# State-space phase of a four-block network: preparation of the next image re-ordered over the steps and partly turned into products on PE, and VectorE's product with C placed between the halves of the next scan

## The reference, cut to what matters

```python
xz = einsum('blc,ec->ble', layer_norm(x), W_in)      # 64 -> 256
xi, z = split(xz)                                     # 128 each
xc = silu(conv_b + sum_k pad(xi)[:, k:k+L] * conv_w[:, k])   # 4 taps along the 1024 positions
dt, Bm, Cm = split(einsum('bld,ed->ble', xc, W_x))    # 4, 16, 16 columns
delta = softplus(einsum('blr,dr->bld', dt, W_dt) + b_dt)
for each position t:                                  # state 128 x 16 per image
    h = h * exp(delta_t * A) + (delta_t * xc_t) * B_t
    y_t = sum over the 16 states of h * C_t
y = (y + xc * Dp) * silu(z)
out = einsum('bld,cd->blc', y, W_out) + x
```

## Time and profile before

| | |
|---|---|
| median of 3 runs | 3678.57 us |
| the profiled execution, its own time | 3668.06 us |
| its span on the core | 3666.4 us |
| busy: PE, DVE, POOL, ACT | 3163.0, 2573.4, 2214.4, 2006.1 us |
| mean granted clock of PE | 0.948 of full |
| first scan of the state-space phase | 2553.05 us into the span |

### The profile page before, as it was taken

One profiled execution on the slowest core, in us unless ns is written; L12 is line 12 of the kernel. 1 busy time (PEld: TensorE's weight loads), 2 busy tenths in 40 slices (PEclk: granted clock), 3 DMA queues, 4 the chain that ended last, 5 costly groups with the idle time before them and its releaser, 6 DMA issues. The chain is left out here.

```text
span 3666.4 us, 55668 instructions
## 1 busy us (share of the span) xinstructions
PE 3163.0 (86%) x18550; PEld 1183.9 (32%) x18550; DVE 2573.4 (70%) x3346; ACT 2006.1 (55%) x2381; POOL 2214.4 (60%) x684
## 2 busy tenths in 40 slices
PE   6999999999999999999995899774888888887787
PEld 2333333333333333333331233341322222222222
DVE  5777777777767777777771222142888988988988
ACT  3566666666656666666663333223555564565554
POOL 0577777777777777777776000003657666666666
PEclk7899999999999999999998999886989999999999
DMA  2000000000000000000003211114333433443443
GB/s 103 12 16 10 16 16 16 16 13 16 16 17 10 16 16 16 19 10 16 16 10 74 92 69 46 48 64 149 119 132 128 155 142 120 153 150 118 147 150 115
DMA packets 74739, 234.86 MB, mean 64 GB/s; under 512 B 13088, under 2 KB 14180, under 8 KB 74420
## 3 DMA queue, kind: packets, MB, share of 16 engines
q1 hardware_dynamic: 69460, 215.06, 17.3%
q0 software_dynamic: 5056, 16.83, 1.3%
HBM read 192.42 MB, written 39.39 MB: 63 GB/s over the span
## 5 line engine op out<-in xcount | busy, mean ns | idle before, releaser
L526 DVE TENSOR_REDUCE at_pmax<-at_ring 128x1 f32<-128x512 f32 x2048 | 1300.8, 685 | 392.0 <-PE at_ring L334 381.2
L479 ACT ACTIVATE at_probs<-at_sc 128x1024 f32<-128x1024 f32 x1024 | 992.5, 1021 | 531.7 <-PE at_sc L402 529.7
L580 POOL TENSOR_TENSOR at_prob_sums<-at_prob_sums,at_probs 128x2048 f32<-128x2048 f32 x256 | 1159.0, 4527 | 74.8 <-ACT at_probs L479 54.5
L398 PE MATMUL at_sc<-at_QT,at_KT 32*128 32x512 f32 x4096 | 782.5, 634 | 4.1 <-issue 3.7
L1634 POOL TENSOR_TENSOR ss_drive<-ss_du,ss_bsb 128x1024 f32<-128x1024 f32 x261 | 610.7, 2352 | 263.9 <-DVE ss_state L1591 257.1
L1534 ACT ACTIVATE ss_decay<-ss_delta,ss_a 128x512 f32<-128x512 f32 x520 | 354.5, 687 | 447.6 <-DVE ss_state L1587 299.5
L410 PE MATMUL at_O<-at_probs,at_V 128*32 128x512 f32 x4096 | 535.3, 606 | 52.5 <-DVE at_att L549 51.6
L580 POOL TENSOR_TENSOR at_prob_sums<-at_probs 128x2048 f32<-128x2048 f32 x64 | 290.7, 4543 | 403.1 <-ACT at_probs L479 403.1
L1423 PE MATMUL ss_Y<-ss_seen,ss_ident 128*128 128x512 f32 x1032 | 520.7, 628 | 0.0
L334 PE MATMUL at_ring<-at_KH,at_QH 32*128 32x512 bf16 x2048 | 442.3, 387 | 5.7 <-DVE at_pmax L526 2.9
L1599 DVE TENSOR_TENSOR ss_seen<-ss_state,ss_C 128x1024 f32<-128x1024 f32 x259 | 316.3, 1221 | 80.4 <-PE ss_C L1411 72.6
(11 more groups left out here) (199 smaller groups left out, 2695.6 us busy)
## 6 DMA issues: line engine op xcount, KB each, us to landing
ss_bsb<-scratch_rows SPq DMA_DIRECT2D x265, 512.0 KB, 6.9
scratch_attn<-at_att SPq DMA_DIRECT2D x64, 256.0 KB, 2.0
fc_att<-scratch_attn SPq DMA_DIRECT2D x32, 512.0 KB, 5.8
ss_xn<-scratch_xm SPq DMA_DIRECT2D x34, 256.0 KB, 5.6
at_xn<-scratch_xn SPq DMA_DIRECT2D x32, 256.0 KB, 3.8
ss_xw<-scratch_xw SPq DMA_DIRECT2D x17, 256.0 KB, 3.9
ln_x<-in_x SPq DMA_DIRECT2D x8, 512.0 KB, 4.2
scratch_xn<-ln_xn POOLq DMA_DIRECT2D x8, 512.0 KB, 3.0
```

The lines of the kernel that those rows point to most:

```text
L398: nc.tensor.matmul(sc[:, h, :], KT[head(h), par, blk(kb)], QT[head(h), par, hs(half)], start=True, stop=False)
L479: nc.scalar.activation(probs[:, kb, two, :].rearrange("p h q -> p (h q)"), sc[:, two, :].rearrange("p h q -> p (h q)"), ACT.Exp, scale=SCA ...
L526: nc.vector.tensor_reduce(pmax[:, quad // 2, h, quad % 2:quad % 2 + 1], ring[:, unit[3], :], AX_X, ALU.max, negate=True).then_inc(max_done, 1)
L580: nc.gpsimd.tensor_tensor(prob_sums[:, half, :, :], before, probs[:, k, :, :], ALU.add).then_inc(pool_sums, 1)
```

## The change

Preparation of image b+1 in the new order (PE: AT_X 5, AT_BC 7, AT_LESS_HI 8, AT_LESS_MID 9, AT_DT 11, AT_Z 13; ACT: AT_PRE 5, AT_U 6, AT_HI 7, AT_MID 8, AT_LOW 9, AT_ABS 11, AT_LN 12, AT_GATE 14; SP writes B at 10, POOL makes delta and du at 13):

- `unit` 1 now makes B and C, `unit` 2 makes delta's input with one 128-row product by `w_delta` = W_x (dt columns) times W_dt, which PE computes once at the start, and `unit` 3 makes z.
- The second and third bf16 parts of B and C are made by PE and ACT: `take_away` repeats the product for B and C and subtracts, with `less` (minus the identity, bf16), the parts that `bc` already holds; ACT copies what is left (`take_mid`, `take_low`). DVE's `take_rest`, ACT's copies of dt and of a second middle part, and POOL's `low` are gone.
- `gate` is made apart from `u_in`, with its own table loads. Softplus is split over ACT's steps 11 and 12.
- DVE runs `see` of step n-1 between the two half scans of step n; Y times gate comes after step 1.
- PE makes the output in two halves, after its steps 1 and 2; ACT still takes it after its decay of step 3.
- The constants are loaded by SP at the end of the loads of the whitening phase; in the state-space phase DVE clears 3 columns of `xn` and the whole of `bc`.

```diff
-def whitening_phase(nc, sem, x_d, total, pair_m, mask_m, ident_m, centred, wm):
+def whitening_phase(nc, sem, x_d, total, pair_m, mask_m, ident_m, centred, wm, load_next):
...
                     sp.dma_start(x[:, u, :], xv[bass.ds(2 * i + u, 1)].rearrange("a p s -> (a p) s")).then_inc(x_in[u], DMA)
+            load_next(sp)
...
+def load_state_space_constants(sp, consts, loaded, w_inT, conv_w, conv_b, w_xT, w_dtT, b_dt, a_log, d_p, w_outT,
+                               select_m, ident_m):
+    w_in, cw, cols, w_x, w_dt, a_neg, w_out, select, ident = consts
+    sp.dma_start(w_in[0:C, :], w_inT).then_inc(loaded, DMA)
+    sp.dma_start(ident[:], ident_m).then_inc(loaded, DMA)
...
-        AT_X, AT_CONV, AT_Z, AT_BC, AT_REST, AT_MID, AT_DT, AT_LOW, AT_DELTA = 6, 6, 8, 9, 10, 11, 12, 12, 13
+        AT_X, AT_BC, AT_LESS_HI, AT_LESS_MID, AT_DT, AT_Z = 5, 7, 8, 9, 11, 13
+        AT_PRE, AT_U, AT_HI, AT_MID, AT_LOW, AT_ABS, AT_LN, AT_GATE = 5, 6, 7, 8, 9, 11, 12, 14
+        AT_ROWS, AT_DELTA = 10, 13
...
 # PE, once
+            nc.tensor.matmul(Y[0:R, 0:DI], w_x[:, 2 * N:], ident[:], start=True, stop=True).then_inc(xr_ready, 1)
+            pe.wait_ge(xr_done, 1)
+            nc.tensor.matmul(Y[:, HALF:HALF + DI], w_xr[:], w_dt[0:R, :], start=True, stop=True).then_inc(delta_w_ready, 1)
 # PE, unit(b, par, k)
                 elif k == 1:
+                    pe.wait_ge(u_done, b + 1)
+                    for h in range(2):
+                        m = nc.tensor.matmul(aux[0:2 * N, hs(h)], w_x[:, 0:2 * N], u_in[:, par, hs(h)], start=True, stop=True)
+                elif k == 2:
+                    pe.wait_ge(low_done, b + 1)
+                    for h in range(2):
+                        m = nc.tensor.matmul(aux[:, hs(h)], w_delta[:], u_in[:, par, hs(h)], start=True, stop=True)
+                else:
+                    pe.wait_ge(relu_done, b + 1)     # then z, as unit 1 before
+            def take_away(b, par, part):
+                if part == 0:
+                    pe.wait_ge(hi_done, b + 1)
+                    pe.wait_ge(brow_done, b + 1)
+                else:
+                    pe.wait_ge(mid_done, b + 1)
+                for h in range(2):
+                    nc.tensor.matmul(aux[0:2 * N, hs(h)], w_x[:, 0:2 * N], u_in[:, par, hs(h)], start=True, stop=False)
+                    for k in range(part + 1):
+                        m = nc.tensor.matmul(aux[0:2 * N, hs(h)], less[:, k, :], bc[:, par, hs(h)], start=False, stop=(k == part))
+                m.then_inc(mid_taken if part else hi_taken, 1)
...
 # PE, in the loop, behind add_state
-                        if now[2] == 1:      # wait for y_step, relu_done, xw_in; both halves of the output
+                        if now[2] in (1, 2):
+                            project_out(b, g, now[2] - 1)   # one half; the first waits for y_step, gate_done, xw_in
...
 # ACT
+            def take_u(b, par):
                 act.wait_ge(pre_done, b + 1)
                 nc.scalar.activation(u_in[:, par, :], pre[:], ACT.Silu).then_inc(u_done, 1)
                 nc.scalar.preload_act_table_set("natural_log_exp_and_others")
+            def take_gate(b, par):
+                act.wait_ge(aux_ready, 4 * b + 4)
+                nc.scalar.activation(gate[:, par, :], aux[:], ACT.Silu).then_inc(gate_done, 1)
+                nc.scalar.preload_act_table_set("natural_log_exp_and_others")
+            def take_hi(b, par):
+                act.wait_ge(aux_ready, 4 * b + 2)        # bc[0:2N] and brow from aux
...
+            def take_mid(b, par):
+                act.wait_ge(hi_taken, b + 1)
+                nc.scalar.activation(bc[2 * N:4 * N, par, :], aux[0:2 * N, :], ACT.Copy).then_inc(mid_done, 1)
+            def take_low(b, par):
+                act.wait_ge(mid_taken, b + 1)
+                nc.scalar.activation(bc[4 * N:6 * N, par, :], aux[0:2 * N, :], ACT.Copy).then_inc(low_done, 1)
...
 # DVE
+            def scan(b, par, n, seen_before):
                 dve.wait_ge(drive_done, b * N + n + 1 + DEPTH)
                 now = state[:, n % 2, :]
+                if not (isinstance(b, int) and n < 2):
+                    dve.wait_ge(seen_done, b * N + n)
                 dve.wait_ge(decay_done, 2 * (b * N + n) + 1)
                 nc.vector.tensor_tensor_scan(now[:, hs(0)], ...).then_inc(first_half_done, 1)
+                if seen_before:
+                    see(*seen_before)
                 dve.wait_ge(first_half_done, b * N + n + 1)
                 dve.wait_ge(decay_done, 2 * (b * N + n) + 2)
                 nc.vector.tensor_tensor_scan(now[:, hs(1)], ...)
...
-                if n == 0:
+                if n == 1:
                     dve.wait_ge(y_ready, (b + 1) * N + DEPTH)
                     nc.vector.tensor_tensor(yv[:], gate[:, par, :], Y[:], ALU.mult).then_inc(y_step, 1)
```

More of the change, by code:

```diff
@@ L1430, in step, with project_out @@
                 spread(Cp, N, b, par, n).then_inc(c_ready, 1)
-                for at, k in ((AT_X, 0), (AT_Z, 1), (AT_BC, 2), (AT_DT, 3)):
+                if n == AT_LESS_HI:
+                    take_away(b + 1, 1 - par, 0)
+                if n == AT_LESS_MID:
+                    take_away(b + 1, 1 - par, 1)
+                for at, k in ((AT_X, 0), (AT_BC, 1), (AT_DT, 2), (AT_Z, 3)):
                     if n == at:
                         unit(b + 1, 1 - par, k)
-            for k in range(4):
-                unit(0, 0, k)
+            def project_out(b, par, h):
+                if h == 0:
+                    pe.wait_ge(y_step, b + 2)
+                    pe.wait_ge(gate_done, b + 2)
+                    pe.wait_ge(xw_in, (b + 1) * DMA)
+                nc.tensor.matmul(aux[0:C, hs(h)], w_out[:], yv[:, hs(h)], start=True, stop=False)
+                m = nc.tensor.matmul(aux[0:C, hs(h)], ident[0:C, 0:C], xw[:, par, hs(h)], start=False, stop=True)
+                m.then_inc(out_ready, 1)
+            unit(0, 0, 0)
+            unit(0, 0, 1)
+            take_away(0, 0, 0)
+            take_away(0, 0, 1)
+            unit(0, 0, 2)
             for n in range(TURN):
@@ L1463, in take_x @@
                 nc.scalar.activation(pre[:], aux[:], ACT.Identity, bias=cols[:, 0:1]).then_inc(pre_done, 1)
-            def gates(b, par):
-                act.wait_ge(aux_ready, 4 * b + 2)
-                nc.scalar.activation(gate[:, par, :], aux[:], ACT.Silu).then_inc(gate_done, 1)
+            def take_u(b, par):
                 act.wait_ge(pre_done, b + 1)
@@ L1538, in step @@
                 make_decay(*ahead(b, par, n, 1))
[L1539 to L1541 removed]
+                if n == 1 and isinstance(b, int):
+                    take_gate(0, 0)
+                if n == AT_PRE:
                     take_x(b + 1)
[L1543 to L1552 removed]
+                if n == AT_U:
+                    take_u(b + 1, 1 - par)
+                if n == AT_HI:
+                    take_hi(b + 1, 1 - par)
+                if n == AT_MID:
+                    take_mid(b + 1, 1 - par)
+                if n == AT_LOW:
+                    take_low(b + 1, 1 - par)
+                if n == AT_ABS:
+                    softplus_in(b + 1)
+                if n == AT_LN:
+                    softplus_log(b + 1)
+                if n == AT_GATE:
+                    take_gate(b + 1, 1 - par)
             make_decay(0, 0, 0)
@@ L1615, in _ @@
                     b = 2 * j + g
+                    before = (b, g, TURN - 1)
                     for now in loop_steps(b, g):
-                        scan(*now)
-                        see(*now)
-                        if now[2] < TURN:
-                            finish(b, g, now[2])
-                        else:
-                            prepare(b + 1, 1 - g, now[2])
+                        scan(*now, before)
+                        before = now
+                        finish(b, g, now[2])
+            see(*before)
         @block.gpsimd
@@ L1651, in step @@
                 make_drive(*ahead(b, par, n, LEAD))
-            low(0, 0)
             make_du(0, 0)
```

196 lines of the change are left out of this document (81 added, 115 removed).

## The result

The changed kernel takes 3744.07 us (median of 4 runs, 3738.42 to 3750.8) beside 3677.08 us (3672.9 to 3679.82) for the kernel before on the same chip: a ratio of 1.0191, 95% interval 1.0177 to 1.0204. It is slower, as forecast, but by 67 us and not by 25, and above the range. The profiled execution spans 3736.7 us (3666.4 before).

What follows compares the result with a forecast made beforehand. DVE was taken to bound the phase, with PE and ACT intruding three times per image. Terms 14 + 12 - 3 + 4 - 2 gave +25 us: 3693 profiled, 3703 as median, with 8 in 10 for 3658 to 3730.

Steps and rivals of the forecast that it cites:

- images, without the clock: State-space phase: an image takes 69.1 us against 68.2 at full clock, +14 us over 15 images.
- PE's clock: PE's products after idle times run at the 1.2 GHz level: 0.8 us per image on average, +12 us.
- start: Phase start: earlier convolution -10, gate off the chain -2, u to Abs +5 to +11, image 0's gate +1.7; together -3 us.
- end and first image: Last image's output ends later, +4 us; the first image escapes more of the waits, -2 us.
- The step of DVE: DVE's scan, product, scan without waiting on the instruction just before: step falls from 3.81 to 3.48 us.
- rival (c): DVE instructions don't overlap, step stays 3.8 us, image 70.3 to 71.7: 3710 to 3731 us; chance 0.13.
- ACT's room falling: ACT's time for preparation between decays shrinks from 3.5 to 2.0 us per step, so DVE waits for decays.
- the time near 3790: With the skill's 2.66 us per ACT table switch, steps 0 and 8 would wait about 2.7 us more each.
- walk: Step-by-step list of DVE's waits for ACT and PE in one image, 12.3 us in sum.
- The late `xn`: SP's input load, behind the store of `res`, lands after PE wants it: 1.3 of step 7's 2.6 us wait.
- (b): Scans release DVE earlier, step 3.25 us, image 68.2 at full clock; chance 0.17 with anything else shortening ACT's waits.
- (a): PE keeps its clock and `xn` lands in time: 67.8 us an image, 3672 us; chance 0.15.

Runs made afterwards that it cites:

- a_busy: Changed kernel plus three pairs of unread idle products per image on PE, behind step 15 and the spreads of steps 1 and 5: 3687.37 us, ratio 1.0062.
- a_xn: Changed kernel with SP issuing the two loads of xn in step 1, ahead of the output's store, instead of step 3: 3673.7 us, ratio 1.0000.
- a_straight: Changed kernel with DVE's order put back to scan, scan, product, and the gate product behind step 0: 3703.29 us, ratio 1.0088.
- b_inter: Kernel before with only DVE's order changed: see of step n-1 between step n's half scans, gate product behind step 1: 3675.0 us, ratio 1.0002.
- a_xn_busy: Changed kernel with the xn loads issued in step 1 and idle PE products behind step 15 and step 1's spread: 3653.05 us, ratio 0.9944.
- a_straight_xn_busy: Changed kernel with DVE's order undone, xn loads in step 1, and one 0.86 us idle product behind each of steps 12, 15, 0: 3599.95 us, ratio 0.9809.

## Why the prediction was right in direction and wrong in size

The terms of the sum, beside what the traces have:

| term | forecast | measured |
|---|---|---|
| images, without the clock | +14 | 15 x 69.5 - 1027.5 = +15.0 |
| PE's clock | +12 | 1101.4 - 15 x 69.5 = +58.9 |
| start | -3 | -9.0 |
| end and first image | +2 | +2.4 |
| phases ahead | 0 | +3.1 |

- The step of DVE: 3.48 forecast, 3.42 measured. The product between the scans takes 1.196 us on average instead of 1.221, and no instruction waits for the end of the one before. So rival (c), the step at 3.8, is refuted. The prediction took a step of 3.8 also from the Trainium skill ("VectorE: DVE Perf Modes", The DRAIN you can't avoid). The same section adds that a next operation that isn't held starts earlier, and these rows agree, by 0.08 to 0.09 us. Its sentence that the semaphore costs nothing extra isn't borne out: an instruction that waits for the one just before it starts 0.04 to 0.13 behind its end.
- ACT's room falling from 3.5 to 2.0 us per step was the right reading: it gave the waits of steps 0, 4, 7, 8, 11 and 13 as 1.7, 3.0, 2.6, 1.5, 1.4 and 0.5. Measured in the two shortest images: 1.68, 2.88, 2.87 to 3.01, 1.45, 1.52, 0.54. That for C in step 2 was 1.6 and is 1.90. A table load still holds ACT for 1.29 us only; the 2.66 of the Trainium skill ("ScalarE: Activation LUTs", What ACT_TABLE_LOAD costs) and the time near 3790 that followed from it are not seen here.
- **The step that failed is the term "PE's clock".** It was put at 0.8 us per image, with +1.7 as its upper end, and measured 3.9. The idle times were named at the right places (3.0 before the spread of step 0, measured 2.88; 2.1 before that of step 4, measured 1.80), and the slack behind step 0 was right: five images have the low clock there, and it costs nothing. What was wrong is the price.
  - The working doesn't hold in itself. A fall over the convolution doubles 3.4 us of products with no slack, by the prediction's own walk, and yet the upper end was 1.7.
  - The convolution takes 5.5 us on average and not 3.6, +1.9 straight into step 7. The idle time ahead of it, for `xn`, had been found in the walk (1.3), but what it does to the clock was not asked.
  - The skip term and the state behind it take 1.9 and 1.2 us longer where the low clock falls on them. Step 2 then waits 4.85 instead of 1.90, on average 3.37, +1.5.
  - These two and step 14 (0.16) make 3.5 of the 3.9. The rest is `xn`, which lands later in most images than in the two shortest.
  - a_busy shows the size without an argument: with nothing but work added, fifteen periods are 1052.5 and not 1101.4 us, -48.9, and the ratio goes from 1.0191 to 1.0062.
- The late `xn` was rightly seen, and wrongly counted as one of many waits. In the image shown the second load is issued 2.9 us behind the end of `res`, as assumed, and PE can start 7.2 after it instead of 5.6. Over the fifteen images the convolution starts 1.5 to 3.2 us later than in a_xn, 2.1 on average, for the walked 1.3. A slow skip term doesn't explain the difference, since DVE's step 4 waits for the same `res` that the load waits for: step 4 always starts 0.6 behind its end and the first load is issued 2.2 to 2.3 behind it. What varies is the time from there to the convolution, 6.0 to 7.8, that is, the landing. a_xn puts its whole price, clock included, at 1.9%, the whole loss.
- The start gained 9.0. Counted from the start of the phase, ACT makes the taps 11.0 earlier (10 was forecast for the convolution); from the taps to u it is 2.9 less; u to Abs cost 2535.67 - 2518.98 = 16.7 for 11.8, +4.9, the lower end of the +5 to +11 of which the middle was taken; and image 0's gate lies behind the first scan, not ahead. The +2.4 of the last row is near the +2 by luck: its parts were +4 and -2, and are +2.4 and 0.
- The phases ahead came out 3.1 us longer, but this varies from one profiled execution to the next: with the same code ahead, `xn` is cleared at 2501.5 in a_straight and 2498.0 in a_busy, and at 2506.9 in b_inter, whose phases ahead are those of before (2501.8). It isn't a cost of the change.
- Of the rivals, (b) was on the right track for the step (3.42, between 3.48 and its 3.25) and wrong for the image. "Clock kept and xn in time" (a), with 3672 or a ratio of 0.998, is nearest to what comes out once both are given: a_xn_busy is at 0.9944, in part by the better start, and a_xn, with the load alone, at 1.0000.

## What to carry to other kernels

Where one engine bounds a loop, making its step shorter takes the same time from every other engine's room: list for each the start it is given and the end it must keep, per step, before counting the gain. A wait found in such a walk has a second price, where it leaves TensorE idle ahead of a chain of products that is itself on the path: count the products behind it at the lower clock, unless they have slack, or fill the idle time. Issue an input load ahead of an output store that has to wait for its data, where both share a queue.

## What the runs showed of the hardware

Products that nobody reads made the kernel faster: a_busy beside after, 1.0062 to 1.0191, and a_straight_xn_busy, with 2.6 us of them per image, 0.9809 to 0.9873. In after the low clock doesn't lie at the same place in every image: behind the same idle time of 2.88 us it lies on the products of step 0 in some and on the skip term 6 us later in others, and one image takes 69.5 and another 77.7 us with the same program. In the kernel before it falls in steps 12 and 13 of every image, and in the first two of the fifteen periods (70.9 and 69.9 us) also on the skip term. Which idle time brings a fall was not settled. In a_straight_xn_busy, with products in three idle places, the clock is at 1.00 (2912 to 3580), while a_busy and a_xn_busy, with others filled, still have six images each with a low clock about step 14.

And on DVE an instruction that doesn't need the one before it starts 0.08 to 0.09 us before that one's end (1.11 after a product of 1.19 or a scan of 1.20), where one that needs it starts 0.04 to 0.13 behind it.
